# Decoder block on one core: operand sums of the seven-product projection built from raw context blocks, stored elsewhere, one used in place, and one product placed ahead of a value projection

## The reference, cut to what matters

```python
x = layernorm(x + self_attention(x))                      # 32 heads of 16, rotary, causal
# cross attention, 32 heads of 128, against a context of 8 x 128 tokens
xn  = rmsnorm(x) * ln_weight
h_q = (xn  @ w_q.T).reshape(b, 128, 32, 128)
h_k = (ctx @ w_k.T).reshape(b, 128, 32, 128)
h_v = (ctx @ w_v.T).reshape(b, 128, 32, 128)
p   = softmax(einsum('bqhd,bkhd->bhqk', h_q, h_k) + position_bias, masked)
x = layernorm(2 * x + einsum('bhqk,bkhd->bqhd', p, h_v) @ w_out.T)
x = layernorm(x + ffn_with_low_rank_experts(x))
```

## Time and profile before

| what | value |
|---|---|
| median of 3 executions | 1098.26 us (1098.13 to 1098.43) |
| the profiled execution | 1096.46 us |
| its span, first to last instruction | 1094.5 us |
| mean granted TensorE clock | 0.988 of full speed |
| busy: PE, DVE, ACT, POOL | 1033.9, 747.5, 500.6, 488.0 us |
| self attention, and its overlap with the first tiles | to about 203 us |
| groups 0 and 1 | to about 318 us |
| groups 2 to 15 | about 51.7 us each |

### The profile page before, as it was taken

One profiled execution on the slowest core, in us unless ns is written; L12 is line 12 of the kernel. 1 busy time (PEld: TensorE's weight loads), 2 busy tenths in 40 slices (PEclk: granted clock), 3 DMA queues, 4 the chain that ended last, 5 costly groups with the idle time before them and its releaser, 6 DMA issues.

```text
span 1094.5 us, 20557 instructions
## 1 busy us (share of the span) xinstructions
PE 1033.9 (94%) x6354; PEld 895.0 (82%) x6354; DVE 747.5 (68%) x2269; ACT 500.6 (46%) x1377; POOL 488.0 (45%) x576
## 2 busy tenths in 40 slices
PE   7899988999689999999999999999999999999995
PEld 6677767888578888888888888888888888888884
DVE  6799988664557575757576666767575757576883
ACT  4889886454324343534343434444343435342421
POOL 7676665799954232423333242423242324232142
PEclk9999999999889999999999999999999999999998
DMA  4301002233375546372727374646455463737001
GB/s 150 126 21 50 2 1 69 78 117 120 124 259 185 193 157 235 115 249 101 258 98 286 99 255 142 242 142 227 164 186 192 157 236 113 249 101 243 19 20 58
DMA packets 44588, 159.77 MB, mean 146 GB/s; under 512 B 4736, under 2 KB 21504, under 8 KB 31616
## 3 DMA queue, kind: packets, MB, share of 16 engines
q0 software_dynamic: 14528, 105.91, 27.3%
q1 hardware_dynamic: 30016, 53.32, 14.5%
HBM read 149.78 MB, written 9.44 MB: 145 GB/s over the span
## 4 chain that ended last, share of the span: by engine, by line
PE 61%; POOL 13%; DVE 9%; DMA 8%; issue 7%; ACT 1%; POOLq 0%; DVEq 0%; SPq 0%; ACTq 0%
PE bank L1940 22%; PE bank L760 13%; PE bank L2094 11%; DMA ring<-block_sums 7%; PE bank L2081 4%; PE bank L2064 4%; PE bank L2112 3%; POOL stage L1053 3%; DVE sm L481 2%; PE bank L2071 2%; POOL u L1053 2%; POOL stage L1061 1%; POOL bm L1045 1%; POOL stage L1057 1%; POOL pool_gate L1070 1%
## 5 line engine op out<-in xcount | busy, mean ns | idle before, releaser
L1045 POOL TENSOR_TENSOR bm<-mask,bias 128x512 f32<-128x512 f32 x64 | 84.0, 1314 | 219.6 <-DVE nmx L1589 217.4
L1334 ACT ACTIVATE pr<-sm,nmx 128x128 f32<-128x128 f32 x256 | 99.8, 391 | 172.2 <-DVE nmx L1589 172.2
L1638 DVE TENSOR_TENSOR acc<-acc,bank 128x512 f32<-128x512 f32 x128 | 86.2, 684 | 78.0 <-PE bank L2094 78.0
L1070 POOL TENSOR_TENSOR pool_gate<-eps 128x1 f32<-128x1 f32 x96 | 44.1, 459 | 186.3 <-PE bank L1940 186.3
L1940 PE MATMUL bank<-ring,wqk_hi 128*128 128x512 f32 x392 | 112.1, 408 | 12.7 <-DMA ring<-block_sums 7.6
L1327 ACT COPY v<-bank 128x256 f32<-128x256 f32 x124 | 45.9, 370 | 127.7 <-PE bank L760 80.8
L2094 PE MATMUL bank<-wo_hi,at_hi 128*128 128x512 f32 x256 | 100.5, 393 | 0.3 <-DVE acc L1638 0.3
L2094 PE MATMUL bank<-wo_hi,at_lo 128*128 128x512 f32 x256 | 100.1, 391 | 0.1
L2094 PE MATMUL bank<-wo_lo,at_hi 128*128 128x512 f32 x256 | 100.0, 391 | 0.0
L1607 DVE TENSOR_TENSOR wqk_lo<-qk_raw,wqk_hi 128x512 fp32r<-128x512 f32 x98 | 88.4, 903 | 10.5 <-ACT wqk_hi L1364 10.5
L760 PE MATMUL bank<-wv_hi,cT_hi 128*128 128x256 f32 x512 | 88.9, 296 | 0.2 <-DVE wv_lo L1895 0.2
(11 more groups left out here) (289 smaller groups left out, 2620.8 us busy)
## 6 DMA issues: line engine op xcount, KB each, us to landing
ring<-block_sums POOLq DMA_DIRECT2D x98, 1024.0 KB, 5.2
qk_raw<-in_wqk SPq DMA_DIRECT2D x56, 256.0 KB, 5.6
o_raw<-in_wo SPq DMA_DIRECT2D x16, 512.0 KB, 3.3
v_raw<-in_wv SPq DMA_DIRECT2D x15, 512.0 KB, 8.7
block_sums<-stage SPq DMA_DIRECT2D x12, 512.0 KB, 3.2
acc<-in_x POOLq DMA_DIRECT2D x1, 2048.0 KB, 8.2
qk_raw<-in_wqk SPq DMA_DIRECT2D x4, 512.0 KB, 5.8
bias<-in_bias SPq DMA_DIRECT2D x16, 128.0 KB, 2.0
```

The source lines that it names most:

```text
L1045: nc.gpsimd.tensor_tensor(bm[:, s % 2], mask[:, HALF * (s // HG):HALF * (s // HG + 1), :], bias[:, i:i + 1, :].broadcast_to([P, HALF, T]), ...
L1070: nc.gpsimd.tensor_tensor(pool_gate[:, BLOCKS.index(name):BLOCKS.index(name) + 1], eps[:, 0:1], eps[:, 0:1], ALU.add)
L1334: e = nc.scalar.activation(pr[:, s % 2, k], sm[:, s % 2, k], ACT.Exp, bias=nmx[:, s % 2, k:k + 1], accum_out=sums[:, s % 2, k:k + 1])
L1638: nc.vector.tensor_tensor(acc[:, b], acc[:, b], PX[b % 2][:], ALU.add).then_inc(s_acc, 1)
```

## The change

It makes the context sums from raw blocks: two DMAs load the raw first token half into areas 0 and 1, as soon as the self attention has left `stage`. The order of the sums and of the mask tiles on POOL is another, the `hi` part of three context sums lies in `mem.u`, and the x sums are in other areas. S2q isn't loaded back for group 2: POOL writes its parts directly into `ring[0]`, and product 6 of q waits for `s_ready`. In step 3 of every group, product 6 of q stands ahead of the first value projection.

```diff
@@ SyncE
+            sp.wait_ge(prev_a.s_wout, B)
+            for i in range(2):
+                sp.dma_start(area(i), mem.context_half(a["cT"], 0)[:, 2 * i:2 * i + 2]).then_inc(s_c_in, 16)
             sp.wait_ge(s_wv, 1)
             load_v(1)
...
-            keep("S1k", stage[:, 0:2 * HALF * T], stage[:, 2 * HALF * T:4 * HALF * T])
-            keep("S2k", stage[:, 0:2 * HALF * T], stage[:, 6 * HALF * T:8 * HALF * T])
+            keep("S1k", u_all, flat[2])
+            keep("S2k", u_all, flat[3])
+            keep("S4k", flat[2], flat[1])
+            keep("S3k", u_all, flat[0])
...
+            keep("S3q", flat[0], flat[3])
+            keep("S4q", flat[0], flat[1])
+            keep("S2q", *[f32(mem.ring[0][:, p].rearrange("p c n -> p (c n)")) for p in range(2)])
@@ GpSimd: the context sums
-            def k_differences():
-                pool.wait_ge(s_clo[0], 2)
-                pool.wait_ge(s_clo[1], 2)
-                combine(area(2), area(2), f32(quarter(cT[0], 0, 0)), ALU.subtract)
-                combine(area(2), area(2), f32(quarter(cT[1], 0, 0)), ALU.subtract)
-                combine(area(3), area(3), area(2), ALU.add)
+            def k_sums():
+                pool.wait_ge(s_clo[0], 2)
+                pool.wait_ge(s_clo[1], 2)
+                pool.wait_ge(s_c_in, 48)
+                combine(area(0), area(2), area(0), ALU.subtract)
+                combine(area(2), area(2), area(3), ALU.add)
+                combine(area(3), area(3), area(0), ALU.add)
+                combine(area(1), area(1), area(3), ALU.subtract)
...
+            def k_second_split():
                 wait_kept(pool, "S1k")
+                hi_of(U_.bitcast(F32R), area(3))
+                block_lo("S2k", area(3, F32R), area(3), U_)
...
+            def q_second_split():
+                wait_kept(pool, "S4q")
+                hi_of(mem.ring[0][:, 0], area(2))
+                block_lo("S2q", mem.ring[0][:, 1], area(2), f32(mem.ring[0][:, 0]))
@@ GpSimd: the order
             bias_mask(0, 2, True)
-            k_differences()
+            k_sums()
             bias_mask(0, 3, True)
-            k_first()
-            k_fourth()
-            k_second()
-            bias_mask(1, 0, False)
+            k_first_split()
+            k_second_split()
             k_fourth_split()
             k_third_split()
+            q_third()
+            bias_mask(1, 0, False)
+            q_second()
             bias_mask(1, 1, False)
-            q_third()
-            q_second()
-            bias_mask(1, 2, False)
             q_third_split()
             q_fourth()
-            bias_mask(1, 3, False)
             q_first()
-            q_second_split()
+            bias_mask(1, 2, False)
             q_fourth_split()
             q_first_split()
-            for name in BLOCKS[-2:]:
-                wait_kept(pool, name)
+            three_turns(SEVEN)
+            q_second_split()
             pool.wait_ge(s_s1q, 1)
-            load_sums(SEVEN, "S2q")
             load_sums(SEVEN, "S2k")
-            three_turns(SEVEN)
+            bias_mask(1, 3, False)
...
+            wait_kept(pool, "S2q")
             second_half(SEVEN)
@@ ScalarE, copy_p1
-                    wait_kept(act, "S2q")
+                    wait_kept(act, "S3k")
@@ TensorE
             def product_6(g, w):
-                pe.wait_ge(s_ring[SLOT_OF[name]], loaded(g, name))
+                if isinstance(g, int) and g == SEVEN and w == 0:
+                    pe.wait_ge(s_ready, 2 * len(BLOCKS))
+                else:
+                    pe.wait_ge(s_ring[SLOT_OF[name]], loaded(g, name))
@@ TensorE, step
                         pe.wait_ge(s_vc, 2 * n + (1 if moved else 3) + j)
+                        if s == 3 and j == 0:
+                            products_between(g, s, j, last, plain, plain_next)
                         project_v(b)
                         if s == 1:
                             products_between(g, s, j, last, plain, plain_next)
                         if j == 0:
                             pv(n - 1, sp, head, v_ready, False)
-                        if s != 1:
+                        if s != 1 and not (s == 3 and j == 0):
                             products_between(g, s, j, last, plain, plain_next)
```

More of the change, by code:

```diff
@@ L827, in layer @@
         SLOT_ORDER = [[n for n in SLOT_OF if SLOT_OF[n] == k] for k in range(2)]
-        BLOCKS = ("S1k", "S2k", "S4k", "S3k", "S3q", "S2q", "S4q")
+        BLOCKS = ("S1k", "S2k", "S4k", "S3k", "S3q", "S4q", "S2q")
         UNITS = ("p1", "p2", "p6", "p5", "p3", "p7", "p4")
@@ L844, in loaded @@
             order = SLOT_ORDER[SLOT_OF[name]]
-            return 16 * len(order) * g + 16 * (order.index(name) + 1 - len(order) * SEVEN)
+            return 16 * len(order) * g + 16 * (order.index(name) + SLOT_OF[name] - len(order) * SEVEN)
         def wait_kept(eng, name):
@@ L995, in _ @@
             load_v(2)
-            keep("S1k", stage[:, 0:2 * HALF * T], stage[:, 2 * HALF * T:4 * HALF * T])
-            keep("S2k", stage[:, 0:2 * HALF * T], stage[:, 6 * HALF * T:8 * HALF * T])
+            u_all = mem.u[:].rearrange("p i n -> p (i n)")
+            flat = [stage[:, k * 2 * HALF * T:(k + 1) * 2 * HALF * T] for k in range(4)]
+            keep("S1k", u_all, flat[2])
+            keep("S2k", u_all, flat[3])
+            keep("S4k", flat[2], flat[1])
+            keep("S3k", u_all, flat[0])
             for i in range(HG):
@@ L1060, in block_lo @@
                 for c in range(2):
-                    nc.gpsimd.tensor_tensor(out[:, c], raw[:, c], f32(hi[:, c]), ALU.subtract).then_inc(s_ready, 1)
+                    nc.gpsimd.tensor_tensor(out[:, c], raw[:, c], hi[:, c], ALU.subtract).then_inc(s_ready, 1)
                     pool.wait_ge(s_ready, 2 * BLOCKS.index(name) + c + 1)
@@ L1108, in q_third, with q_second @@
                 combine(area(3), f32(quarter(xnT[0], 0, 1)), f32(quarter(xnT[0], 0, 0)), ALU.subtract)
+                combine(area(3), area(3), f32(quarter(xnT[1], 0, 1)), ALU.add)
+                combine(area(3), area(3), f32(quarter(xnT[1], 0, 0)), ALU.subtract)
+            def q_second():
                 wait_kept(pool, "S4k")
-                combine(area(1), f32(quarter(xnT[1], 0, 1)), f32(quarter(xnT[1], 0, 0)), ALU.subtract)
-                combine(area(3), area(3), area(1), ALU.add)
@@ L1113, in q_second @@
-            def q_second():
-                combine(U_, area(3), f32(quarter(xnT[0], 1, 1)), ALU.add)
-                combine(U_, U_, f32(quarter(xnT[1], 1, 1)), ALU.add)
+                combine(area(2), area(3), f32(quarter(xnT[0], 1, 1)), ALU.add)
+                combine(area(2), area(2), f32(quarter(xnT[1], 1, 1)), ALU.add)
             def q_third_split():
```

48 lines of the change are left out of this document (15 added, 33 removed).

## The result

The changed kernel took 1126.41 us (1122.91 to 1130.93), the kernel before 1098.2 us beside it: 1.026 times as long, interval 1.0224 to 1.03. It is slower, as forecast, but by 28 us and not by 5. The profiled execution took 1122.91 us, with a span of 1121.0 us, 26.5 us more than before.

A forecast was written before the change was run, and what follows sets the result against it. It took PE to bound the kernel nearly everywhere. The entry's +4.2 us and the loop's +0.9 us, summed to +5.1 us and put on the median, gave 1103.4 us; the 8-in-10 range was 1090 to 1107.5 us.

The forecast's parts named there:

- The bound and the sign: Whole kernel: PE is the bound nearly everywhere, and the change makes it slower, chance 0.50.
- The entry: Entry into group 2: POOL's longer chain makes the scores of tile 8 later by 4.2 us (0 to +7).
- The ring loads for group 2 stay in time ... no price: End of the entry: S1k can go at 314, is asked for at 323.6; S2q's store blocks POOL until about 310.
- The loop: Seven-product groups: S1k's wait goes, S4k is late instead; nine groups lose 0.16, four gain 0.14; +0.9 us (-11 to +3).
- the landing of S4k: Loop: S4k, issued 4.16 us after the scores and taking 6.0, lands at +10.16; product 3 of k starts at +10.26.
- The wait for S1k: Loop, product 5 of k: S1k, late by 0.85 us at most, is issued 2.3 us earlier, so the wait goes.
- and nothing asks for them in step 3: Loop, step 3: `pv` and the output it feeds come 1.4 us later, with no reader there waiting for them.
- S4k in 6.0 us: Loop: S4k's load takes 6.0 us, sized by group 5, where a weight load follows 0.2 us behind its issue.
- S4k in 5.1 us: Loop rival: with S1k and S4q out of its way, S4k loads faster; 10.9 us gained, 1091.6 us; chance 0.25.
- POOL's chain shorter: Entry rival: POOL's chain 3 to 5 us shorter, clock holds; entry -1 to 0, no change, 1098 us; chance 0.17.
- the late mask costs little: Entry rival: mask tile 4's lateness costs little, both PE waits go, half of 16.7 us saved, 1090 us; chance 0.08.

The follow-up runs named there:

- e2: The changed kernel with the old order of product 6 of q restored in every group; 1104.03 us, ratio 1.0063.
- e8: The changed kernel with T1 ahead of at_hi and at_lo, T3's low part behind the sum of w, mask tiles 4 and 7 early; 1093.99 us.
- e7: e2 with mask tile 4 moved into POOL's wait for the store of S1k, ahead of the split of S2k; 1100.97 us.
- e3: The kernel before with only the loop's new order of product 6, and T1's parts ahead of at_hi and at_lo; 1102.76 us, ratio 1.0050.
- e12: The kernel before with the loop's new order, loads of a, c and v held until product 3 of k is done; 1088.12 us in one execution.
- e13: The changed kernel with the loads of a, c and v held until product 3 of k is done; 1096.4 us, ratio 0.9992.
- e16: The kernel before, old order kept, with the loads of a, c and v held until product 3 of k is done; 1088.94 us, ratio 0.9934.
- e5: e3 with T3's low part also moved behind the sum of w on DVE; 1087.58 us, ratio 0.9918.
- e6: e2 with mask tile 7 moved right behind mask tile 6 on POOL; 1104.12 us, ratio 1.0063.
- e9: e8 with SP's load of the third group's bias ahead of the keeping of S2q; 1087.98 us, ratio 0.9919.

## Why the prediction was right or wrong

**The bound and the sign** were right: PE's time grew by its waits, on the side that got the largest chance, slower. The sign is not luck, since the entry alone makes the kernel slower (e2, +7.1 us). The size was wrong: 28 us, not 5.

**The entry** was forecast at +4.2 us (0 to +7) and came at +6.9 for the scores of tile 8. Its steps held. The raw loads were in at 217.0 (216.0 forecast), `k_sums` took 13.9 us (13.6), the wait for the store of S1k 4.08 (4.0), mask tile 4 was ready at 262.9 (261.8), PE idled 13.94 us (12.9) and 5.07 us (4.0), product 6 of q started at 313.41 (311.2), and from there to the scores 12.1 us (11.6). The 2.7 us over the forecast are 1.8 of POOL's chain (mask tile 7 ready at 308.3, not 306.5), 0.4 from there to product 6 of q, and 0.5 behind it. "The ring loads for group 2 stay in time ... no price" was right for the changed kernel: S1k went out at 317.95 and took 5.1 us, and product 5 of k followed the scores after 0.81 us, without a wait. But it was closer than laid out. The store of S2q was in at 311.9, not 310, and behind it stood the load of the third group's bias, which the forecast didn't have; mask tile 8 waited for it until 314.13. This became a price only when the chain ahead of it was shortened, in e8. That the 13.9 us of idle time is not a price of its own, since POOL's chain sets the end, is what e7 showed.

**The loop** was forecast at +0.9 us (-11 to +3) and came at some +19.5. This is the step that failed, and the range with it: the landing of S4k, forecast 10.16 us after the scores, was at 11.4 on average (4.32 + 7.09) and at 12.3 in the worst groups. The wait for S1k went, as forecast, and S4k's issue was at +4.32 (+4.16). Two sentences were wrong. The first, that `pv` and what it feeds come 1.4 us later "and nothing asks for them in step 3": T1's parts stand behind `at_hi` and `at_lo` on ACT and DVE, and behind T1 SP's loads of 1 MB of weights. The prediction looked at each product's own readers and not at what is queued behind them on ACT, DVE and SP. The second followed from it, S4k in 6.0 us: it was sized by group 5, where d's load comes 0.2 us behind it, but where S4q and v are in earlier, 5.6 and 5.0 us after the scores.

With a, c and v back in their place (e3) S4k took 6.2 to 6.4 us, so that figure was fair for what it counted; in the changed kernel it took 7.1 on average. S4q and v, which went out together, were still in flight when S4k started, until +6.3 and +6.6; before they were in at +5.8 and +5.4. That alone doesn't give the size in each group: in group 7 S4q was in at +6.76 and S4k took 6.2 us, in group 9 it was in at +6.96 and S4k took 8.0. That the weight loads do it is shown by holding them (e12, e13: 5.0 to 5.3 us in every group); how the loads share the engines from group to group is not shown. S4q's own delay, up to 0.63 us at product 3 of q in six groups, had no term in the sum at all. The clock, which fell behind the longest waits, made it larger: each step 0 was 2.56 us over 13.4, of which waits are about 21.4 / 12 = 1.8. The wait for S1k, which the forecast took to be mended by an earlier issue, was such a collision itself (e16).

**The rivals.** *S4k in 5.1 us* was the right picture of the loop without collisions: it put 10.9 us on it, and e5, where S4k takes 5.2 us, gains 12 x (14.32 - 13.43) = 10.7 there and 8.6 in its time. It is not what the order is worth, since the old order with the weights held (e16) gains nearly as much. The rule weighed there, from the Trainium skill, "DMA: Bandwidth & Descriptors", section "Anatomy of one DMA — SWDGE (gpsimd) path", gives an estimate of 4.4 us. The trace differs: 5.0 to 5.6 us for 1 MB in the runs with the weight loads held, and the rule has no term for another load in flight. Another section of that page, "Queues, rings and completion order", does: every DMA engine takes turns, packet by packet, between the queues that have work for it. The trace agrees as far as it goes: S4q and v, issued 0.3 us apart on two queues, took 9.0 and 8.8 us, where S4q takes 5.0 to 5.3 with the weights held (e12, e13). It doesn't show single turns.

*POOL's chain shorter* did not happen: mask tile 7 was ready at 308.3, 1.8 us later than laid out. Neither did *the late mask costs little*.

## What to carry to other kernels

A load's time in the trace of before holds only for what was in flight beside it. Before an edit that moves an instruction by a microsecond, follow the queue behind it on every engine to the DMAs that it releases, and set them against the loads that are waited for. Where loads have slack, tie their issue to the landing of the one that has none: here one wait ahead of the weight loads was worth 6 us to the kernel before and 30 us to the changed one, and with it the two orders of the products came within 0.5 us of each other.

## What was not expected of the hardware

- Loads of 1 MB that take 5.0 to 5.6 us with the weight loads held took up to 9.5 us beside 256 and 512 KB weight loads.
- A load of 128 KB behind a store of 1 MB, with a load of 1 MB from the other queue in flight and one of 512 KB behind it, took 5.7 us (changed kernel), 7.3 (e8) and 9.0 (e6). A load of the same size took 2.1 us near 233 us in e2's profile. In e9, where only the store stood ahead of it and no load was beside it, it took 4.0 us; the shares of the others were not tried apart.
- DVE's 128x512 subtraction of two SBUF tiles took 4.72 us instead of 0.68 beside three POOL instructions of 1.25 to 1.27 us that followed each other without a gap, and ended 0.6 us after the last of them. The Trainium skill, "SBUF — State Buffer", section "Who interferes with whom", says that DVE and POOL share a port pair, that a DVE instruction with two SBUF inputs contends for it with a POOL instruction that reads SBUF, and that whichever is issued first holds it to its end while the other engine is blocked. The trace agrees only in part: DVE's instruction started at 308.09, 0.46 us ahead of the first of the three, POOL's ran at their usual length, and DVE's lasted over all of them and not over one. It was seen once and not tried by itself.
